# Layer 1's expert lists collected by GpSimd, its router weights scaled by ScalarE

## The reference

```
x = x + L0_xattn(layernorm(x), ctx)      # 8 heads, rotary, softmax, output projection
x = x + L0_ffn(layernorm(x))             # router, top 8 of 64, silu(g) * u, down
x = x + L1_xattn(layernorm(x), ctx)      # 8 heads, no rotary, no output projection
x = x + L1_ffn(layernorm(x))
# L1_ffn: probs = softmax(x @ router); topw, topi = top_k(probs, 8); topw /= topw.sum()
#         the (token, expert) pairs in the order of tokens; an expert takes its first CAP = 128
#         out[token] += topw * expert(x[token])
```

## Time and profile before

| | |
|---|---|
| median of 3 runs | 2065.82 us (2065.47 to 2069.38) |
| the profiled execution | 2065.41 us, of which 2063.7 us from its first to its last instruction |
| busy | PE 81%, DVE 68%, ACT 61%, POOL 48% |
| attention of layer 0 / experts of layer 0 | about 0 to 620 us / 650 to 1110 us |
| attention of layer 1 (41 steps) | about 1140 to 1820 us |
| experts of layer 1 | about 1820 to 2064 us |
| a full step of layer 1 (steps 9 to 32) | 19.08 us, the same within 0.02 us but for two steps (19.38 and 19.28 us) |

### The profile page before, as it was taken

One profiled execution on the slowest core, in us unless ns is written; L12 is line 12 of the kernel. 1 busy time (PEld: TensorE's weight loads), 2 busy tenths in 40 slices (PEclk: granted clock), 3 DMA queues, 4 the chain that ended last, 5 costly groups with the idle time before them and its releaser, 6 DMA issues. The chain is left out here.

```text
span 2063.7 us, 45000 instructions
## 1 busy us (share of the span) xinstructions
PE 1665.0 (81%) x12724; PEld 1130.1 (55%) x12879; DVE 1412.1 (68%) x4335; ACT 1264.0 (61%) x3300; POOL 985.5 (48%) x1114
## 2 busy tenths in 40 slices
PE   3999999999973999999997268888888888845651
PEld 1555555555543789888986134444444444444530
DVE  5888888888854455545434469999999999743330
ACT  1777677777761566666665258888888887621210
POOL 4367677777763000000001666666666663148883
PEclk9999999999995999999999589999999999969896
DMA  5678877777736966666665578898778876178856
GB/s 139 160 210 243 224 213 213 210 211 216 202 119 185 346 213 202 198 198 201 196 199 160 138 187 202 227 233 199 194 195 200 195 195 151 51 187 186 177 93 111
DMA packets 413088, 390.98 MB, mean 189 GB/s; under 512 B 46640, under 2 KB 385072, under 8 KB 412848
## 3 DMA queue, kind: packets, MB, share of 16 engines
q1 hardware_dynamic: 341888, 259.97, 47.3%
q0 software_dynamic: 37904, 90.22, 17.6%
q10 hardware_dynamic: 33056, 37.90, 6.2%
HBM read 233.74 MB, written 170.16 MB: 196 GB/s over the span
## 5 line engine op out<-in xcount | busy, mean ns | idle before, releaser
L1086 DVE TENSOR_REDUCE mx<-psS 128x2 f32<-128x512 f32 x1024 | 678.9, 674 | 112.3 <-PE psS L1479 72.5
L886 ACT ACTIVATE prob<-psE 128x512 f32<-128x512 f32 x1024 | 601.1, 595 | 227.6 <-PE psE L1492 211.6
L741 POOL DMA_INDIRECT yg<-y_d,row_all x256 | 249.7, 975 | 642.7 <-SPq L401 484.1
L1492 PE MATMUL psE<-q,k 128*128 128x256 bf16 x2048 | 395.2, 275 | 38.8 <-ACT prob L886 16.1
L1479 PE MATMUL psS<-k,q 128*128 128x512 bf16 x869 | 337.0, 390 | 32.8 <-DMA k<-k_stack_d 26.2
L1602 PE MATMUL psE<-wt,xgT 128*128 (+1 forms) x1536 | 325.8, 336 | 6.1 <-ACT xgT L984 5.6
L1431 DVE TENSOR_TENSOR hid<-sil,psE 128x96 f32<-128x96 f32 x384 | 97.6, 254 | 333.0 <-ACT sil L989 332.8
L728 POOL DMA_INDIRECT xs_d<-xr,row_all x256 | 252.6, 987 | 109.3 <-ACT prob L886 65.4
L1492 PEld LDWEIGHTS psE<-q,k 128*128 128x128 bf16 x2048 | 186.0, 98 | 194.3 <-ACT prob L886 70.6
L1508 PE MATMUL psO<-prob,v 128*32 128x256 f32 x4096 | 275.9, 387 | 8.5 <-ACT osb L866 8.5
L984 ACT COPY xgT<-psS 128x256 f32<-128x256 f32 x384 | 144.5, 376 | 197.4 <-PE psS L1596 137.5
(11 more groups left out here) (219 smaller groups left out, 2632.4 us busy)
## 6 DMA issues: line engine op xcount, KB each, us to landing
xg<-xs_d SPq DMA_DIRECT2D x320, 128.0 KB, 2.6
y_d<-y_all SPq DMA_DIRECT2D x320, 128.0 KB, 2.3
q<-q_stack_d SPq DMA_DIRECT2D x128, 256.0 KB
k<-k_stack_d SPq DMA_DIRECT2D x128, 256.0 KB
wt<-in_gu ACTq DMA_DIRECT2D x128, 192.0 KB, 3.7
q_stack_d<-parts SPq DMA_DIRECT2D x64, 192.0 KB
k_stack_d<-parts SPq DMA_DIRECT2D x64, 192.0 KB
wt<-in_dn ACTq DMA_DIRECT2D x128, 96.0 KB, 4.2
```

Source lines behind the costliest of these rows:

```text
L741: g.indirect_dma_start(yg[:, k, :], None, y0_d[:, :], bass.IndirectOffsetOnAxis(row_all[:, row(st.pair("load") * K + k, 1)], 0))\
L886: a.activation(prob[gr][:, u % 4, :], psE[ring][:, :], ACT.Exp, scale=SCALE).then_inc(s_exp, 1)
L1086: v_.tensor_reduce(mx[b][:, bg // 4, :].rearrange("p (h r) -> p h r", h=2)[:, :, (bg % 4) * 2 + tt], psS[(UNITS * (st.s0 - LAG["smax"]) + ...
L1492: ins = m_.matmul(psE[ring][:, i * T:(i + 1) * T], k2[b][:, bg, hh * T + i * P:hh * T + (i + 1) * P], q2[b][:, bg, :], start=True, stop=True)
```

## The change

DVE loses the two additions into `id_acc` and the scaling of the weights. ACT gets two instructions: in unit 9 of steps 8 to 39 the product of `exm` and the reciprocal, behind a wait for DVE's reciprocal (semaphore `s_wk`), and in unit 15 of steps 9 to 40 a copy of the list product (128x128) from PSUM to a new tile `lst`, behind a wait for GpSimd's last use of `lst` (`s_ids`). This copy now frees the `psM` bank. GpSimd gets three instructions of 128x64: one scales half of `lst` by the pair's number, one adds the other half to `id_acc`, one, behind a wait for the first two, adds the scaled half. They stand behind the second gather of the step after, and those of the last step behind the whole loop and ahead of the barrier. `lists()` waits for them.

```
+            def ids(st):
+                if not st.on("post"):
+                    return
+                done = st.n1("post", 3, 0)
+                pool.wait_ge(s_list, st.n1("post"))
+                if done:
+                    pool.wait_ge(s_ids, done)
+                g.tensor_scalar(lst[:, 0:E], lst[:, 0:E], float(P * st.pair("post")), None, ALU.mult).then_inc(s_ids, 1)
+                g.tensor_tensor(id_acc[:, :], id_acc[:, :], lst[:, E:2 * E], ALU.add).then_inc(s_ids, 1)
+                pool.wait_ge(s_ids, done + 2)
+                g.tensor_tensor(id_acc[:, :], id_acc[:, :], lst[:, 0:E], ALU.add).then_inc(s_ids, 1)
...
                         for k in range(K):
                             gather(st, k, PACE[L][k])
+                            if k == 1:
+                                ids(Step(1, st.s0 - 1))
...
                 if L == 0:
                     for b in range(NB):
                         pool.wait_ge(d_sent[b], 16 * K * uses_of(b))
+                else:
+                    ids(Step(1, STEPS - 1))
                 barrier(pool, 2 + 2 * L)
...
+                    if L == 1 and u == 15 and st.on("post"):
+                        act.wait_ge(s_lsp, st.n1("post"))
+                        wait(act, s_ids, st.n1("post", 3, 0))
+                        a.copy(lst[:, :], psM[item_bank(1, "LIST")][:, 0:2 * E]).then_inc(s_list, 1)
+                    if L == 1 and u == 9 and st.on("place"):
+                        act.wait_ge(s_wk, st.n("place"))
+                        a.mul(xr[st.buf("place")][:, T:T + E], exm[:, :], den[:, 1:2]).then_inc(s_wall, 1)
...
-                        ch.add(v_.reciprocal(den[:, 1:2], den[:, 0:1]), "inv")
+                        if L == 0:
+                            ch.add(v_.reciprocal(den[:, 1:2], den[:, 0:1]), "inv")
+                        else:
+                            v_.reciprocal(den[:, 1:2], den[:, 0:1]).then_inc(s_wk, 1)
...
-                            v_.tensor_scalar(xr[b][:, T:T + E], exm[:, :], den[:, 1:2], None, ALU.mult)\
-                              .then_inc(s_wall, 1)
...
-                    if L == 1 and u == 15 and st.on("post"):
-
-                        ps = psM[item_bank(1, "LIST")]
-                        dve.wait_ge(s_lsp, st.n1("post"))
-                        wait(dve, s_list, st.n1("post", 1, 0))
-                        ch.add(v_.scalar_tensor_tensor(id_acc[:, :], ps[:, 0:E], float(P * st.pair("post")), id_acc[:, :],
-                                                       ALU.mult, ALU.add), "ids")
-                        ch.join("ids")
-                        v_.tensor_tensor(id_acc[:, :], ps[:, E:2 * E], id_acc[:, :], ALU.add).then_inc(s_list, 1)
...
             def lists():
 
+                dve.wait_ge(s_ids, 3 * PAIRS)
```

More of the change, by code:

```diff
@@ L316, in build @@
         expert_at = ab("expert_at", [P, E])
+        lst = ab("lst", [P, 2 * E])
         hotr = ab("hotr", [P, K, P], BF16)
@@ L384, in build @@
         s_sum, s_match = sem("s_sum"), sem("s_match")
+        s_ids = sem("s_ids")
         s_chain = sem("s_chain")
@@ L1228, in body @@
                         ch.join("den")
-                        ch.add(v_.reciprocal(den[:, 1:2], den[:, 0:1]), "inv")
-                    if u == 9 and st.on("place"):
-                        b = st.buf("place")
-                        ch.join("inv")
[L1233 to L1236, removed]
-                            v_.tensor_scalar(xr[b][:, T:T + E], exm[:, :], den[:, 1:2], None, ALU.mult)\
-                              .then_inc(s_wall, 1)
+                        if L == 0:
+                            ch.add(v_.reciprocal(den[:, 1:2], den[:, 0:1]), "inv")
+                        else:
+                            v_.reciprocal(den[:, 1:2], den[:, 0:1]).then_inc(s_wk, 1)
+                    if u == 9 and st.on("place") and L == 0:
+                        ch.join("inv")
+                        v_.tensor_scalar(w_all[:, row(st.pair("place"), K)], ex[:, 0:K], den[:, 1:2], None,
+                                         ALU.mult).then_inc(s_wk, 1)
                     if L == 0 and u == 4 and st.on("front"):
```

## The result

The changed kernel takes 2079.28 us (median of 5 runs, 2077.35 to 2079.74), against 2066.85 us for the kernel before on the same chip: a ratio of 1.0058, 95% interval 1.0045 to 1.0071, or 12 us more. The direction was forecast, the size was twice the forecast of +6.0. The profiled execution took 2079.28 us, its span is 2077.6 us against 2063.7.

The account below looks back on a forecast made before the run. DVE's path from unit 8 to the next unit 0 was taken as the later by 0.10 us over PE and ACT's. Terms 3.8 + 0.7 + 1.5 = +6.0 us on the median 2065.82 gave 2071.8 us, range 2064.0 to 2080.0.

Parts of the forecast that it names:

- Two paths, 0.10 us apart, and the product on the later one: Unit 8 to next unit 0: DVE's 8.02 us against PE and ACT's 7.92, becoming 8.17; +0.15 us each full step.
- DVE is the bound: Rival, chance 0.10: PE's path shortens as DVE is earlier, the full 0.53 us gained in some 25 steps; 2054 us.
- ACT absorbs the product: Rival, chance 0.18: PE has unseen air between unit 11's exponential and unit 13's tile, the product costs nothing; 2064.7 us.
- ACT's price of 0.25 us: ACT's weights product in unit 9 takes 0.25 us of its queue, ends 0.19 and 0.30.
- the gathers absorb it: 0: GpSimd's three instructions, about 1.2 us, fit its air ahead of the seventh gather and behind `rem`; cost 0.
- the 0.73 us behind `rem`: GpSimd stands at least 0.73 us more for ACT behind `rem`, counted as air for its new instructions.
- GpSimd becomes late: Rival, chance 0.08: DVE holds GpSimd's instructions over 1.9 us, eating the air and lengthening each step; 2086 us.
- DVE beside GpSimd, 0.03 a step: Units 4 and 5, GpSimd's instructions holding DVE's: 0.03 us a step, ends 0 and 0.24, in 24 steps +0.7.
- The instructions seem to miss each other but for a touch: GpSimd's new operations and DVE's in units 4 and 5 hardly overlap; reason for taking 0.03 us a step.
- The last steps and the end, +1.5: Steps 36 to 40: +0.5 at step 40's start, the end chain about 1.6 instead of 0.62; ends 0.8 and 2.5.
- Step 33: Full step without DVE's sums, where PE's path was already the later one: +0.25 us.
- All high ends together (2079.2): 24 x (0.20 + 0.24) + 0.3 + 2.5 = +13.4 us, giving 2079.2.

Follow-up runs that it names:

- weights alone: Kernel before with only the weights' scaling moved from DVE to ACT in unit 9: ratio 1.0026 in the second series, 1.0056 on another chip.
- lists alone: Changed kernel with the weights scaled by DVE as before: ratio 1.0010 in the second series, 0.9936 on another chip.
- relief of DVE alone: Kernel before without the two list additions and the weights' scaling, on no engine: ratio 1.0003, step 32 18.99 us.
- lists early: Changed kernel with GpSimd's list instructions ahead of the first gather, the last ones behind the barrier: ratio 1.0031.
- all moved: As lists early, plus ACT's weights ahead of unit 8's exponential and its `hote` product in unit 7: 2055.80 us, 0.9954 of before.
- second series: Runs of weights alone, lists alone, lists early and all moved, where the kernel before took 2065.29 us (24 runs).

## Why the prediction was right, and where it was too small

- **Two paths, 0.10 us apart, and the product on the later one: right.** The step of 19.26, PE's 8.16 us with the weights alone, 7.92 with the lists alone, 18.99 for the relief of DVE alone. "DVE is the bound" (2054 us) is refuted by the latter, though DVE was busy 96% of the time. "ACT absorbs the product" is refuted by the weights alone.
- **ACT's price of 0.25 us: right.** Measured 0.25; the nearest row said 0.26. The estimate of 0.24 from the Trainium skill (ScalarE: Activation LUTs, What ACT_TABLE_LOAD costs) agrees.
- **GpSimd's three instructions, "the gathers absorb it: 0": the step that failed.** In the quiet steps it holds. But I took the 1.17 us of air as free because it was idle in the step I looked at the earlier trace rows. It was also the reserve for two 3.0 us stalls, which stand in the trace of before as the rows above show, and which I did not look for. One of them is in step 14, the very step from whose end I took the 0.73 us behind `rem`; in a quiet step of before it is 1.50. The rival "GpSimd becomes late" had the right chain, from eaten air to a late `rem`, but expected it in every step and from slow list instructions; they took 1.3 us of GpSimd's time. Price: steps 14 and 15 together +3.6, 28 and 29 +0.9, less the 0.18 of each as a quiet step: 3.8 (some 0.2 of it, in step 15, is the contention of the next point).
- **DVE beside GpSimd, 0.03 a step: too small.** Right in steps 18 to 27. In steps 10 to 13, 16 and 17 it is a further 0.18 to 0.33 us, so 0.21 to 0.36 in all, around and above my upper end of 0.24. "The instructions seem to miss each other but for a touch" had no row behind it, since the new starts could not be read from the trace of before; shifts of 0.04 us and more in them changed it. With the lists early, the extra is 0.05 us. The rule of the Trainium skill (SBUF — State Buffer, Who interferes with whom), that the two exclude each other, agrees: `exm` takes 0.43 us where GpSimd's instruction starts as `ys` ends, and 0.22 where GpSimd comes 0.05 us later.
- **The last steps and the end, +1.5: mis-sized.** Steps 33 to 39 and the end came to 4.61 (+0.95 and +3.66), where I had 1.85 (1.5 and the 0.35 of the steps 33 and 36). Step 33 itself was right: +0.23 for +0.25. The chain of copy and three instructions was right. The 2.72 us between GpSimd's last instruction and the open barrier were missing, since in the kernel before GpSimd had long been done there. `hote` behind the weights costs 1.67 us in steps 38 and 39 with the weights alone; without DVE's additions 0.78 of it is left in the changed kernel.
- **The sum** of the forecast with these three terms (+3.8 for the stalls, +1.5 for the steps 10 to 17, +2.8 for the end) is 14.1 us, against 13.9 between the profiled spans, in which a further +1.1 ahead of step 9 and -1.4 in the experts' stage nearly cancel. All high ends together (2079.2) come within 0.1 us of the result, but by the wrong terms: no end covered the stalls or the barrier. The direction was right by its mechanism; that 2079.28 still lies within the range up to 2080.0 is luck.

## What to carry to other kernels

Where two paths run side by side, taking work from the busiest engine pays only down to the other path, and giving that work to the other path's engine makes the kernel slower. Place it where the receiving engine waits: the same product made the step some 0.25 us longer in unit 9 and 0.02 us in unit 7, and with both paths cut the step fell by 0.46 us. Before air on an engine is spent, look over all steps at what it absorbs now, and prefer the air that comes ahead of the irregular event's place to the only air behind it. Look again once the step has become shorter: in all moved the stalls cost 2.1 us.

## What the hardware showed that I had not expected

- GpSimd stands for 2.8 to 3.0 us ahead of one gather in step 14 and one in step 28, in both kernels compared and in all four of the second series (2.76 us in step 28 of two of them), with nothing in the profile that accounts for it.
- The barrier opens 2.72 us behind GpSimd's last computing instruction, in six kernels of six. In the kernel before, where GpSimd had nothing to compute late, the next stage began 0.1 us behind DVE's last addition (1819.66 + 0.22 = 1819.88).
- Of DVE's `exm` and GpSimd's first list instruction, 0.05 us in GpSimd's start decided between 0.43 and 0.22 us for `exm` (steps 17 and 19). It is no simple threshold: with starts 0.04 to 0.2 us later than in the quiet step, `exm` took 0.34 us in steps 10, 11 and 13.
- On two other chips the same kernel takes 5% longer, with engines standing for up to 3 us and more nearly once a step, and the relation of two versions can turn round there: lists alone was 1.0010 of before on the one chip and 0.9936 on the other.
